# A three-pass decoder layer on one core: products with v in two groups, expert products of 512 columns, one bias product, and half of the masks added on VectorE

## The chip, the cores and the metric

One core of one Trainium2 chip. The metric is device time of one execution in microseconds (us). TensorE does matrix products and transposes, VectorE and ScalarE elementwise work and reductions, GpSimd elementwise work and the causal select; SyncE only issues transfers.

## What is computed

32 sequences of 128 tokens with 256 features, in fp32. Three residual blocks, each closed by a layer norm:

```
x = layernorm(x + causal self-attention(x))                    # 16 heads of 16
x = layernorm(x + cross-attention(x, ctx, mask))               # 16 heads of 16
x = layernorm(x + self-attention(x) + mixture(x))              # 8 experts, top 2

expert_out = einsum('bsd,edf->bsef', x, W_experts) + b_experts
mixture    = einsum('bsef,bse->bsf', expert_out, combine)      # combine: top-2 gate values, else 0
```

All 8 experts are computed for every token and weighted by `combine`.

## The kernel before

The work is cut in items of two sequences (256 tokens): 16 items, each taken through three passes (the code's layers 0, 1, 2), so n runs from 0 to 47. All tokens stay in `x_all` between the passes. The work of an item overlaps with that of its neighbours: each step has a written time in `TIMES` for each pass, an item starts `PERIOD` after the one before, and every engine's queue is the steps of its own, sorted by these times (`ORDER`, L125). Nothing is planned at run time: the order is fixed, semaphores hold each step until its inputs are there, and a step that waits holds all behind it on its engine. Only the order follows from the written times; no instruction waits for a time.

One item, in order of its data:

- x in feature-major form is split in a high part of the matmul's reduced type and a low rest (`xh`, `xl`; for ctx `ch`, `cl`). Products with weights are three passes, high x high, high x low, low x high, in `three_pass` (recorded as L429), each 128 x 128 against 256 columns.
- q and k (`q`, `k`) go through ScalarE and GpSimd into bf16 parts, which SyncE stacks by transfers in `q_stack` and `k_stack` (three buffers of each; the zeros and ones between the rows are set once at the start by `clear_stacks`, L765, on VectorE).
- First scores (`s1`, `max_scores`, L489): for each of 8 head pairs four bf16 products of 128 columns fill a bank (two banks take turns), and in the passes with a mask a fifth, identity by mask with 512 columns (L505), adds the mask. VectorE reduces the bank to four columns of negated row maxima (`max`, `row_max`, L849). When all 8 pairs are done VectorE splits the maxima in parts (`nm`, L857), TensorE transposes them (`maxt`, L513), ScalarE copies them (`mt`, L699), a transfer adds them to the stack (`ml`).
- Second scores (`s2`, `scores`, L526): transposed and with the maxima subtracted by the product; the second pass adds its mask by a product (L529). ScalarE takes the exponential (`exp`, L707) into one of four `probs` buffers; in the first pass GpSimd zeroes what lies above the diagonal (`causal`, L1004).
- Products with v (`pv`, `values`, L533): four parts per item, each of two head pairs: 16 fp32 products with 32 weight columns on four column tiles, 128 columns each. A part waits for the exponential (first pass: the causal select) of its second pair. Two parts fill a work bank, which ScalarE copies (`za`) to one of two `z_aug` buffers; TensorE transposes it (`zT`), VectorE divides by the sums (`z`).
- Passes one and two: transpose, split, output product (`zt`, `zh`, `zl`, `out`), residual and norm (`sum`, `rs`, `norm`).
- Pass three: a gate on VectorE (`gtop`, down to L844), transposed (`gateT`) and copied (`cbt`); the bias product (`bias`, L590), two fp32 products of 8 rows against 256 columns; then the experts. Unit e is expert e for both sequences: 12 products of 256 columns, `[128, 256]` per sequence (`expert`, L593); VectorE adds each sequence's half to x with its weight, two independent instructions (`combine`, L925). z is added by `zadd` (L936), then the norm.

The four work banks are handed out by `assign_banks` (L152) from the written times. Weights of later passes are loaded in eight pieces during the first two. At the start VectorE clears the three stacks, makes the first weights' low halves and the constants; ScalarE's later work waits for these constants (`setup_v`).

## Time and profile before

| | us |
|---|---|
| three runs | 1025.30 to 1025.67, median 1025.55 |
| the profiled execution, its own time | 1025.35 |
| its span | 1023.6 |
| granted TensorE clock, mean | 0.991 |

| engine | busy share | instructions |
|---|---|---|
| TensorE, products | 93% | 11008 |
| TensorE, weight loads | 80% | 11008 |
| VectorE | 75% | 2092 |
| ScalarE | 52% | 1083 |
| GpSimd | 39% | 486 |

Busy time counts an engine's instructions while they run; TensorE's are pipelined, so the distance from one start to the next is its cost in the queue, not its duration. "Idle before" is the time in which the engine had nothing running ahead of an instruction. A span contains everything from the first instruction to the last; the device time is a little longer.

### The profile page before, as it was taken

What the parts mean: (1) busy time and instruction counts of PE and PEld (TensorE: products, weight loads), DVE (VectorE), ACT (ScalarE), POOL (GpSimd) and SP (SyncE); (2) the same over time, 40 slices, a digit from 0 to 9 for tenths busy, and PEclk for the clock granted to TensorE, in tenths of its full rate; (3) what the DMA queues carried; (4) which work ended last, traced back from release to release, by engine and by line L of the source; (5) the groups of instructions that cost most, each with busy time, mean ns of one, the idle gap of its engine ahead of it and who ended that gap; (6) DMA issues with size and microseconds to landing.
All of it is one profiled execution on the core that took longest, in us unless ns stands there. A gap on an engine that the chain in (4) does not pass through costs nothing.

```text
span 1023.6 us, 28458 instructions
## 1 busy us (share of the span) xinstructions
PE 950.7 (93%) x11008; PEld 817.3 (80%) x11008; DVE 763.3 (75%) x2092; ACT 537.1 (52%) x1083; POOL 396.6 (39%) x486
## 2 busy tenths in 40 slices
PE   2889888989999999999999999999999999999996
PEld 2677777878777777877778779999999999999985
DVE  7467667677766678677676678888888888888885
ACT  3456666757665566565665654444444444444422
POOL 2567767676756243352342522222222222222200
PEclk8899999999999999999999999999999999999999
DMA  4654554545444343343342422222222222222200
GB/s 145 164 143 125 138 146 123 151 124 157 117 114 123 99 126 105 85 126 95 96 114 75 125 64 64 64 75 79 75 73 64 78 75 75 63 77 78 73 28 22
DMA packets 98134, 100.85 MB, mean 99 GB/s; under 512 B 10696, under 2 KB 90576, under 8 KB 98000
## 3 DMA queue, kind: packets, MB, share of 16 engines
q1 hardware_dynamic: 98000, 99.03, 34.9%
q8 instruction: 88, 1.44, 0.6%
q14 instruction: 46, 0.38, 0.1%
HBM read 18.51 MB, written 4.19 MB: 22 GB/s over the span
## 4 chain that ended last, share of the span: by engine, by line
PE 61%; DVE 17%; POOL 14%; issue 5%; ACT 2%; DMA 0%; DVEq 0%; POOLq 0%; ACTq 0%
PE work L429 35%; PE work L547 6%; POOL probs L1004 6%; PE scores L526 6%; PE max_scores L502 5%; DVE neg_max L849 5%; DVE x_all L901 3%; PE work L556 2%; PE max_scores L505 2%; POOL k_parts L967 2%; POOL x_all L989 2%; PE scores L529 2%; POOL q_parts L967 2%; PE work L590 2%; DVE x_all L925 1%
## 5 line engine op out<-in xcount | busy, mean ns | idle before, releaser
L849 DVE TENSOR_REDUCE neg_max<-max_scores 128x4 f32<-128x512 f32 x384 | 256.8, 683 | 105.0 <-PE max_scores L505 86.3
L707 ACT ACTIVATE probs<-scores 128x512 f32<-128x512 f32 x384 | 226.6, 596 | 202.4 <-PE scores L526 158.2
L960 POOL TENSOR_TENSOR q_full<-q_full,q_parts 128x512 f32<-128x512 f32 x48 | 56.9, 1186 | 338.7 <-ACT q_parts L663 338.7
L526 PE MATMUL scores<-q_stack,k_stack 128*128 128x128 bf16 x1536 | 151.0, 221 | 2.0 <-DMA q_stack<-neg_max_t 1.1
L502 PE MATMUL max_scores<-k_stack,q_stack 126*128 126x128 bf16 x1536 | 150.1, 220 | 1.6 <-DVE neg_max L849 1.6
L547 PE MATMUL work<-probs,v_ones 128*32 128x128 f32 x3072 | 123.7, 279 | 23.8 <-POOL probs L1004 22.3
L429 PE MATMUL work<-w_hi,split_hi 128*128 128x256 f32 (+1 forms) x448 | 138.0, 308 | 1.0
L429 PE MATMUL work<-split_hi,w_hi 128*128 128x256 f32 x384 | 118.0, 307 | 19.5 <-DVE split_lo L758 19.5
L526 PEld LDWEIGHTS scores<-q_stack,k_stack 128*128 128x128 bf16 x1536 | 97.0, 98 | 44.5 <-issue 19.2
L925 DVE SCALAR_TENSOR_TENSOR x_all<-work,combine,x_all 128x256 f32<-128x256 f32 x256 | 110.8, 474 | 27.0 <-PE work L429 24.8
L502 PEld LDWEIGHTS max_scores<-k_stack,q_stack 126*128 126x128 bf16 x1536 | 104.8, 97 | 30.0 <-issue 8.9
L429 PE MATMUL work<-w_lo,split_hi 128*128 128x256 f32 (+1 forms) x448 | 126.9, 283 | 0.0
L429 PE MATMUL work<-w_hi,split_lo 128*128 128x256 f32 (+1 forms) x448 | 126.4, 282 | 0.0
L547 PEld LDWEIGHTS work<-probs,v_ones 128*32 128x32 f32 x3072 | 72.4, 109 | 60.5 <-POOL probs L1004 26.7
L429 PE MATMUL work<-split_lo,w_hi 128*128 128x256 f32 x384 | 110.4, 288 | 0.0
L429 PE MATMUL work<-split_hi,w_lo 128*128 128x256 f32 x384 | 110.3, 287 | 0.0
L505 PE MATMUL max_scores<-mask_qk,ident_b 128*128 128x512 bf16 x256 | 97.8, 382 | 0.0
L1004 POOL TENSOR_SCALAR_AFFINE_SELECT probs<-probs 128x512 f32<-128x512 f32 x128 | 81.8, 646 | 28.0 <-ACT probs L707 26.5
L429 PEld LDWEIGHTS work<-split_hi,w_hi 128*128 128x128 f32 x384 | 75.0, 195 | 21.4 <-DVE split_lo L758 19.8
L429 PEld LDWEIGHTS work<-w_hi,split_hi 128*128 128x128 f32 x448 | 84.9, 190 | 4.4 <-DVE split_lo L761 4.1
L429 PEld LDWEIGHTS work<-w_lo,split_hi 128*128 128x128 f32 x448 | 84.9, 190 | 0.4
L429 PEld LDWEIGHTS work<-w_hi,split_lo 128*128 128x128 f32 x448 | 84.7, 189 | 0.0
(105 smaller groups left out, 2100.5 us busy)
## 6 DMA issues: line engine op xcount, KB each, us to landing
q_stack<-q_parts SPq DMA_DIRECT2D x288, 128.0 KB, 2.4
k_stack<-k_parts SPq DMA_DIRECT2D x288, 128.0 KB, 2.4
in_t<-in_xt SPq DMA_DIRECT2D x16, 256.0 KB, 2.9
x_all<-in_x SPq DMA_DIRECT2D x16, 256.0 KB, 2.9
in_t<-in_ct SPq DMA_DIRECT2D x16, 256.0 KB, 2.6
out<-x_all SPq DMA_DIRECT2D x16, 256.0 KB, 2.1
stage<-in_e SPq DMA_DIRECT2D x4, 512.0 KB, 5.2
stage<-in_qk SPq DMA_DIRECT2D x2, 512.0 KB, 4.0
```

Of the source, the lines that this page charges most:

```text
L429: mm = pe.matmul(dst, a(c), b(c), start=(c == 0 and k == 0), stop=(c == C - 1 and k == 2))
L502: mm = pe.matmul(dst[:, b, h2, :], head(QS, n, 2 * p + h2, b, ROWS), head(KS, n, 2 * p + h2, b, ROWS), start=(b + h2 == 0), stop=(b + h2 = ...
L505: mm = pe.matmul(dst[:, :, :, :], IDB[:, :], MQ[l][:, :].unsqueeze(1).to_broadcast([P, 2 * PB, P]), start=False, stop=True, skip_group_che ...
L526: mm = pe.matmul(dst[:, b, h2, :], head(KS, n, 2 * p + h2, b, rows), head(QS, n, 2 * p + h2, b, rows), start=(b + h2 == 0), stop=(b + h2 = ...
L547: mm = pe.matmul(dst[o:o + QUAD, (p % 4) * P:(p % 4 + 1) * P], VA[n % VALUES][:, b, (2 * p + h2) * VH:(2 * p + h2) * VH + QUAD], PR[S2_TUR ...
L707: act.activation(PR[g % PROBS][:, :, :, :], SS[g % 2][:, :, :, :], ACT.Exp).then_inc(probs_done, 1)
L849: dve.tensor_reduce(NM[n % 2][:, :, 2 * p:2 * p + 2], SM[g % 2][:, :, :, :], AX.X, ALU.max, negate=True).then_inc(max_read, 1)
L901: ins = dve.tensor_scalar(x[:, b, :], x[:, b, :], MV[:, l, b, 0:1], RS[:, l, b:b + 1], ALU.subtract, ALU.mult)
L925: ins = dve.scalar_tensor_tensor(out=x[:, b, :], in0=src[:, b * D:(b + 1) * D], scalar=CB[n % 2][:, b, e:e + 1], in1=x[:, b, :], op0=ALU.m ...
L960: pool.tensor_tensor(FULL[x][:, :, :], FULL[x][:, :, :], PART[x][:, 0, :, :], ALU.subtract).then_inc(rest_done[x], 1)
L967: pool.tensor_tensor(PART[x][:, 2, :, :], FULL[x][:, :, :], PART[x][:, 1, :, :], ALU.subtract).then_inc(low_done[x], 1)
L1004: pool.affine_select(probs, probs, [[0, 2 * PB], [1, P]], ALU.is_ge, 0.0, base=0, channel_multiplier=-1).then_inc(causal_done, 1)
```

## The change

Five parts, and new written times for every step (so the order of steps on each engine changes in many places; only a few are shown).

1. In passes one and two the mask product is left out for pairs 1, 3, 5 and 7. For these VectorE runs four instructions over 128 columns in place of one reduction over 512: add the mask (bf16, in SBUF) to the scores (in PSUM), times -1, running minimum into the maxima's column; the sum is written back over the scores.
2. Products with v come in two groups of four pairs. Probabilities and `z_aug` share six buffers, given out by the written times, in place of four and two.
3. An expert unit is two experts for one sequence: 6 products of 512 columns. Its two accumulations on VectorE go to the same part of x, and the second waits for the first.
4. The expert bias is multiplied in the reduced type as one product per sequence over 24 rows (high by high, high by low, low by high), in place of fp32 over 8 rows. The gate makes the three copies of its weights; the bias parts are made at the start.
5. At the start GpSimd clears the first two stacks, VectorE the third, each as 2048 words of 32 bits; TensorE runs six fp32 products of 512 columns ahead of its first work. Products with weights wait for their own low part.

```diff
+MAX_DVE = ((1, 3, 5, 7), (1, 3, 5, 7))
...
-PERIOD = [16.5, 17.99, 25.01]
+PERIOD = [16.49, 18.06, 25.0]
@@ TIMES, first pass
...
-     "max": [-16.18, -14.72, -13.26, -11.81, -10.35, -8.9, -7.45, -5.94], "nm": [-5.11], "maxt": [-4.53],
-     "exp": [0.17, 1.58, 3.0, 4.41, 5.83, 7.24, 8.66, 10.08], "pv": [3.93, 6.65, 9.36, 11.91], "za": [7.67, 12.96],
-     "norm": [31.53], "causal": [0.97, 2.38, 3.8, 5.21, 6.63, 8.04, 9.46, 10.88]},
+     "max": [-16.13, -13.83, -13.7, -12.06, -10.44, -8.46, -7.83, -4.97], "nm": [-4.02], "maxt": [-3.71],
+     "exp": [1.97, 2.98, 4.02, 4.84, 6.34, 8.28, 9.13, 9.34], "pv": [8.35, 12.36], "za": [9.01, 13.36],
+     "norm": [31.78], "causal": [3.37, 4.0, 5.26, 5.55, 7.46, 9.26, 9.62, 10.17]},
@@ TIMES, second pass
...
-     "max": [-16.26, -14.84, -13.44, -12.01, -10.59, -9.18, -7.77, -6.3], "nm": [-5.95], "maxt": [-5.21],
+     "max": [-17.1, -14.78, -13.95, -11.6, -11.1, -8.71, -7.24, -6.13], "nm": [-5.75], "maxt": [-3.27],
@@ TIMES, third pass
...
-     "rs": [23.83], "norm": [25.03], "store": [25.5]},
+     "rs": [32.15], "norm": [33.9], "store": [25.9]},
...
+ATTN_BUFS = 6
+def assign_buffers():
+    slot, before = {}, {}
+    free_at, last = [-1e9] * ATTN_BUFS, [None] * ATTN_BUFS
+    for t, kind, n, part in ORDER:
+        if kind not in ("exp", "za"):
+            continue
+        j = min((i for i in range(ATTN_BUFS) if free_at[i] <= t), key=lambda i: free_at[i])
+        slot[(kind, n, part)], before[(kind, n, part)] = j, last[j]
+        free_at[j] = WHEN[("pv", n, part // 4) if kind == "exp" else ("zT", n, part)] + 0.01
+        last[j] = (kind, n, part)
+    return slot, before
...
+            pe.wait_ge(setup_p, 1)
+            for _ in range(6):
+                pe.matmul(WB[WORK_BANKS - 1][0:QUAD, :], VA[0][:, 0, 0:QUAD], VA[0][:, :, 0:2 * P], start=True, stop=True)
...
             def max_scores(n, p):
+                added = l < 2 and p not in MAX_DVE[l]
...
-                if l < 2:
+                if added:
                     mm = pe.matmul(dst[:, :, :, :], IDB[:, :], MQ[l][:, :].unsqueeze(1).to_broadcast([P, 2 * PB, P]),
                                    start=False, stop=True, skip_group_check=True)
...
-            def values(n, j):
+            def values(n, f):
...
-                    pe.wait_ge(causal_done, S2_TURN[(n, 2 * j + 1)] + 1)
+                    pe.wait_ge(causal_done, S2_TURN[(n, 4 * f + 3)] + 1)
...
-                for p in (2 * j, 2 * j + 1):
+                for p in range(4):
...
-                    mm = pe.matmul(dst[:, b * D:(b + 1) * D], CBT[0:E, b * P:(b + 1) * P], EB[:, :], start=True, stop=True)
+                    mm = pe.matmul(dst[:, b * D:(b + 1) * D], CBT[0:BIAS_ROWS, b * P:(b + 1) * P], EBP[:, :],
+                                   start=True, stop=True)
...
-            def expert(n, e):
+            def expert(n, u):
+                g, b = divmod(u, PB)
...
+                mm = three_pass(mine("expert", n, u)[:, :],
+                                lambda c: hi[:, c, b * P:(b + 1) * P], lambda c: lo[:, c, b * P:(b + 1) * P],
+                                lambda c: wh[:, c, o:o + width], lambda c: wl[:, c, o:o + width])
...
-            clear_stacks(0).then_inc(stacks_clear, 1)
             first_low(0)
             x_low(0, 0)
-            clear_stacks(1).then_inc(stacks_clear, 1)
...
+            setup_link(dve.tensor_copy(EBH[:, :], EB[:, :]))
+            setup_link(dve.tensor_tensor(EBH[:, :], EBH[:, :].bitcast(F32), LOW_ROWS.to_broadcast([BIAS_ROWS, D]), ALU.mult))
+            dve.tensor_tensor(EBP[:, :], EB[:, :], EBH[:, :].bitcast(F32), ALU.subtract)
...
-            clear_stacks(2).then_inc(stacks_clear, 1)
+            dve.memset(pairs_of(QS[2]), 0.0)
+            dve.memset(pairs_of(KS[2]), TWO_ONES).then_inc(last_stack_clear, 1)
...
-                dve.tensor_tensor(cb[:, :, 0:E], G1[:, :, :], G2[:, :, :], ALU.add).then_inc(combine_done, 1)
+                dve.tensor_tensor(cb[:, :, 0:E], G1[:, :, :], G2[:, :, :], ALU.add)
+                dve.tensor_tensor(cb[:, :, E:2 * E], G1[:, :, :], G2[:, :, :], ALU.add)
+                link(dve.tensor_tensor(CBH[:, :, :], G1[:, :, :], G2[:, :, :], ALU.add))
+                dve.tensor_tensor(cb[:, :, 2 * E:3 * E], cb[:, :, 0:E], CBH[:, :, :].bitcast(F32),
+                                  ALU.subtract).then_inc(combine_done, 1)
...
             def row_max(n, p):
+                l = layer(n)
+                if l < 2 and p in MAX_DVE[l]:
+                    for b in range(PB):
+                        for h2 in range(2):
+                            h, scores = 2 * p + h2, SM[g % 2][:, b, h2, :]
+                            ins = dve.tensor_tensor_reduce(scores, scores, MQ[l][:, :], -1.0, HUGE, ALU.add, ALU.min,
+                                                           NM[n % 2][:, b, h:h + 1])
...
-            def combine(n, e):
+            def combine(n, u):
+                g, b = divmod(u, PB)
...
+                for half in range(2):
+                    e = 2 * g + half
+                    ins = dve.scalar_tensor_tensor(out=x, in0=src[:, half * D:(half + 1) * D], scalar=CB[n % 2][:, b, e:e + 1],
+                                                   in1=x, op0=ALU.mult, op1=ALU.add)
+                    if half == 0:
+                        link(ins)
...
@@ GpSimd, at the start
+            for j in range(2):
+                pool.memset(pairs_of(QS[j]), 0.0)
+                pool.memset(pairs_of(KS[j]), TWO_ONES).then_inc(stacks_clear, 1)
             pool.wait_ge(setup_v, 1)
```

## Rows read from the trace of the kernel before

**Rows 1.** The page's first part: busy us (share of the span) and instructions.

```profile
PE 950.7 (93%) x11008; PEld 817.3 (80%) x11008; DVE 763.3 (75%) x2092; ACT 537.1 (52%) x1083; POOL 396.6 (39%) x486
```

**Rows 2.** Windows by pass: length, busy of PE, PEld, DVE, ACT, POOL.

```profile
0.00:38.35 38.35, 16.28 (x103) 13.66 (x103) 27.06 (x35) 13.08 (x22) 11.74 (x16) 0.87 0.51 155
38.35:315.30 276.95, 250.47 (x3145) 210.74 (x3144) 187.71 (x469) 179.12 (x343) 193.85 (x252) 0.99 0.49 134
315.30:612.50 297.20, 283.59 (x3366) 228.49 (x3366) 214.92 (x525) 179.34 (x355) 111.37 (x129) 1.00 0.37 102
612.50:998.40 385.90, 383.65 (x4205) 349.64 (x4205) 320.31 (x1021) 158.97 (x353) 77.88 (x86) 1.00 0.25 69
```

**Rows 3.** Windows, same cut, of L699 alone (one per item).

```profile
612.50:998.40 385.90, 5.58 (x15) 1.00 0.25 69
```

**Rows 4.** Waits of PE in the first and the second pass: us, times, longest.

```profile
PE work L547 <- POOL probs L1004: 22.0, 20, 1.4
...
PE work L513 <- DVE neg_max_parts L858: 10.9, 14, 0.9
```

**Rows 5.** Timeline of PE in the first pass: start us, us, instruction.

```profile
253.45 0.38 PE L505 MATMUL max_scores<-mask_qk,ident_b 128*128 128x512 bf16 x1
253.67 0.39 PE L526 MATMUL scores<-q_stack,k_stack 128*128 128x128 bf16 x4
```

**Rows 6.** Timeline of PE, third pass, around products with v.

```profile
791.53 0.40 PE L502 MATMUL max_scores<-k_stack,q_stack 126*128 126x128 bf16 x4
791.86 0.65 PE L547 MATMUL work<-probs,v_ones 128*32 128x128 f32 x16
792.44 0.40 PE L526 MATMUL scores<-q_stack,k_stack 128*128 128x128 bf16 x4
792.67 0.39 PE L502 MATMUL max_scores<-k_stack,q_stack 126*128 126x128 bf16 x4
792.87 0.37 PE L429 MATMUL work<-w_hi_experts,split_hi 128*128 128x256 f32 x1
793.08 0.28 PE L429 MATMUL work<-w_lo_experts,split_hi 128*128 128x256 f32 x1
793.20 0.28 PE L429 MATMUL work<-w_hi_experts,split_lo 128*128 128x256 f32 x1
```

**Rows 7.** Windows inside that group, products with v alone.

```profile
791.85:791.95 0.10, 0.09 (x4) 0.09 (x8) 1.00 0.48 154
791.95:792.06 0.11, 0.11 (x8) 0.11 (x12) 1.00 0.26 84
```

**Rows 8.** Timeline of PE, third pass, around the bias products.

```profile
813.87 1.12 PE L590 MATMUL work<-expert_bias,combine_t 8*128 8x256 f32 x4
814.93 0.40 PE L502 MATMUL max_scores<-k_stack,q_stack 126*128 126x128 bf16 x4
```

**Rows 9.** Groups of VectorE: count | busy us, mean ns | idle.

```profile
L849 DVE TENSOR_REDUCE neg_max<-max_scores 128x4 f32<-128x512 f32 x384 | 256.8, 683 | 105.0 <-PE max_scores L505 86.3 <-PE max_scores L502 16.7
...
L925 DVE SCALAR_TENSOR_TENSOR x_all<-work,combine,x_all 128x256 f32<-128x256 f32 x256 | 110.8, 474 | 27.0 <-PE work L429 24.8
...
L870 DVE TENSOR_TENSOR z<-work,z_recip 128x128 f32<-128x128 f32 x192 | 46.9, 286 | 3.3
...
L844 DVE TENSOR_TENSOR combine<-combine_first,combine_second 128x16 f32<-128x16 f32 x16 | 2.8, 175 | 0.6
```

**Rows 10.** Timeline of VectorE in the third pass.

```profile
791.14 0.49 DVE L870 TENSOR_TENSOR z<-work,z_recip 128x128 f32<-128x128 f32 x2
...
793.01 1.28 DVE L849 TENSOR_REDUCE neg_max<-max_scores 128x4 f32<-128x512 f32 x2
```

**Rows 11.** Chain that ended last, its start: start us, us.

```profile
3.86 3.47 DVE k_stack L767
...
24.33 0.64 DVE split_lo L758
...
29.73 0.24 PE max_scores L502 x4
```

More of the change, by code:

```diff
@@ L180, in last_reader @@
 def last_reader(name, n):
-    if layer(n) == 2:
-        return "expert", n, E - 1
-    return ("q" if layer(n) == 1 and name == "x" else "v"), n, 0
+    pieces = {0: [("q", 0), ("k", 0), ("v", 0)], 1: [("q", 0)] if name == "x" else [("k", 0), ("v", 0)],
+              2: [("q", 0), ("k", 0), ("v", 1), ("expert", E - 1)]}[layer(n)]
+    kind, part = max(pieces, key=lambda piece: WHEN[(piece[0], n, piece[1])])
+    return kind, n, part
 SPLIT_BEFORE = {}
@@ L313, in bank_read, with attn, attn_free @@
             eng.wait_ge(done, n + 1 if once else turn(n) if reader == "ve" else count(reader, n, rpart))
+        def attn(kind, n, part):
+            return AT[ATTN_SLOT[(kind, n, part)]]
+        def attn_free(eng, kind, n, part):
+            use = ATTN_BEFORE[(kind, n, part)]
+            if use is None:
+                return
+            before, m, mpart = use
+            if before == "za":
+                eng.wait_ge(z_psum[mpart], m + 1)
+            else:
+                eng.wait_ge(pv_psum, PV_TURN[(m, mpart // 4)] + 1)
         def bank(kind, n, part=0):
@@ L323, in split_free @@
             kind, m, part = last_reader(*use)
-            done = {"expert": e_psum, "q": psum["q"], "v": v_psum[0]}[kind]
-            eng.wait_ge(done, count(kind, m, part) if kind == "expert" else m + 1)
+            done = {"expert": e_psum, "q": psum["q"], "k": psum["k"], "v": v_psum[part % PB]}[kind]
+            eng.wait_ge(done, count(kind, m, part) if kind == "expert" else turn(m) if kind == "v" and part else m + 1)
         def pair(n):
@@ L346, in decoder @@
         CONSTS = 5
-        S2_PIECE = {j: piece for piece, j in S2_TURN.items()}
         block = stack.enter_context(nc.Block())
@@ L502, in max_scores @@
                         mm = pe.matmul(dst[:, b, h2, :], head(QS, n, 2 * p + h2, b, ROWS), head(KS, n, 2 * p + h2, b, ROWS),
-                                       start=(b + h2 == 0), stop=(b + h2 == 2 and l == 2), skip_group_check=True)
-                if l < 2:
+                                       start=(b + h2 == 0), stop=(b + h2 == 2 and not added), skip_group_check=True)
+                if added:
                     mm = pe.matmul(dst[:, :, :, :], IDB[:, :], MQ[l][:, :].unsqueeze(1).to_broadcast([P, 2 * PB, P]),
@@ L921, in combine @@
                 for f in range(2):
[L922 removed]
+                    if WHEN[("zadd", n, f)] < WHEN[("combine", n, u)]:
                         dve.wait_ge(zadd_done[f], turn(n))
[L924 to L927 removed]
+                for half in range(2):
[4 more added lines that the diff above has]
+                        link(ins)
                 ins.then_inc(e_done, 1)
```

119 lines of the change are left out of this document (61 added, 58 removed), and 44 rows, old and new, of the table TIMES.

## The prediction

> **What bounds the kernel now.** The page's busy line gives TensorE 950.7 us of matmul in a span of 1023.6 us, VectorE 763.3, ScalarE 537.1, GpSimd 396.6 [rows 1]. The reader should not stop there: these are means over three passes. I cut the trace at the transposes of the maxima, one per item, into a start, three stretches (one per pass) and an end, and read the busy time of each [rows 2]; the same cut counts 16, 16 and 15 items, of which the last count is shown [rows 3]. So an item takes 276.95/16 = 17.3 us in the first pass, 297.2/16 = 18.6 us in the second and 385.9/15 = 25.73 us in the third; the start is 38.35 us and the end 25.2 us. VectorE is busy for 187.7/16 = 11.7, 214.9/16 = 13.4 and 320.3/15 = 21.4 us of an item, GpSimd for 193.9/16 = 12.1 us in the first pass.
>
> The waits of TensorE in those stretches say what is left over [rows 4]: in the first pass 22.0 us for the causal select on GpSimd ahead of the products with v, in the second 10.9 us for the parts of the maxima from VectorE, in the third nearly nothing (busy 383.65 of 385.9). TensorE's queue thus sets the pace everywhere: about 17.3 - 22.0/16 = 15.9 us of work per item in the first pass, 18.6 - 10.9/16 = 17.9 in the second, 25.7 in the third. What leaves its queue comes off the time, until VectorE, the next one, is full.
>
> **The masks.** In the first two passes each pair's bank of maxima scores gets four 128-column products and a 512-column product that adds the mask. From its start to the start of the next product that mask takes 253.67 - 253.45 = 0.22 us [rows 5]. Pairs 1, 3, 5 and 7 lose it: 4 x 0.22 = 0.88 us per item, 128 instructions, 28 us in all. In return VectorE does, for these pairs, four instructions over 128 columns (add the mask, negate, running minimum, sum written back to PSUM) in place of one maximum over 512. Two of those maxima back to back take 1.28 us, that is 0.64 to 0.67 each [rows 9, 10]. No row shows the new instruction. The nearest one is the 128-column multiply out of PSUM, 286 ns alone but 0.49 us for two, 0.245 each [rows 10]. The other end is the three-operand accumulation, 110.8/256 = 0.433 us over 256 columns back to back [rows 9]; with 128 columns fewer at the slope between 0.245 (128 columns) and 0.67 (512), 1.1 ns a column, it is 0.29, and its full 0.474 us bounds it above. I take 0.27: the kind is that of the first row with a second operation and an accumulator. Four are 1.08 us, 0.41 us more than the maximum, so 1.6 us per item and 53 us of VectorE in all. Bounds: 0.245 (1.2 us per item) and 0.474 (4.9 us).
>
> By the Trainium skill ("VectorE: DVE Perf Modes", on where the cycles go for N = 2048) every Vector instruction pays some 158 cycles beside its elements at 0.96 GHz, which speaks against splitting one into four: (128 + 158)/0.96 = 298 ns, 1.19 us for four, so by that estimate VectorE gets 2.1 us per item; the pair of multiplies at 0.245 us each disagrees when instructions follow one another.
>
> **The products with v.** Per item four groups of 16 become two of 32. A group of 16 takes 792.44 - 791.86 = 0.58 us to the next product's start, and the product ahead of it is at 0.33 us instead of 0.23 [rows 6]. Inside the group four column tiles start together each 0.11 us: 4 are seen in the first window and 8, four of them new, in the next [rows 7]. So 32 take about 0.58 + 4 x 0.11 = 1.02 us, against 1.16, and one entry of 0.10 goes too: 0.24 per merged group, 0.46 us per item in every pass. The wait is now for four pairs of probabilities instead of two; six shared buffers instead of four plus two hold them, and the written order puts the first product with v later (8.35 on the first pass's clock, where the causal select of the pair it needs stands at 5.55; before, 3.93 and 2.38). The distance grows from 1.5 to 2.8, and for the last group from 1.0 to 2.2. The transpose of the maxima, too, gets 2.5 behind the making of its parts in the second pass instead of 0.7. Both waits of [rows 4] should mostly go.
>
> **The experts.** A unit now is 12 products of 256 columns, 0.12 us apart (793.08 to 793.20) with 0.09 more at the first [rows 6]: 1.43 us. It becomes 6 products of 512 columns. No row has a wide product of this type; two narrow ones bound it above at 0.24, the wide bf16 mask at 0.22 is nearest and I take it: 1.32 us, 0.11 less per unit, 8 units, 0.88 us per item. The bound below is that a wide one comes at the step of a narrow one, 0.12. The two accumulations on VectorE now depend on each other and a wait stands between them; where two now take 0.87, I count 0.474 x 2 + 0.04 = 0.99: 0.12 x 8 = 0.9 us of VectorE per item (bounds 0 and 1.6).
>
> By the Trainium skill ("TensorE: Matmul & The Clock Gate", Back-to-back issue gap) a sustained stream of weight loads and products goes at about 131 ns for 512 columns. The mask in this trace takes 0.22 us and so disagrees.
>
> **The bias.** The four records of the fp32 product take 814.93 - 813.87 = 1.06 us plus an entry of 0.10 [rows 8]. Two products of 256 columns in the type of the experts are 0.24 + 0.09: 0.83 us less per item. VectorE gets three small operations and a link, at 0.175 us each [rows 9]: 0.5 us, ahead of the gate's transpose, which already stands behind other work.
>
> **Sum for the middle.** TensorE per item: first pass 15.9 - 0.88 - 0.46 = 14.6; second 17.9 - 1.34 = 16.6; third 25.7 - 0.46 - 0.88 - 0.83 = 23.6. VectorE: 11.7 + 1.6 = 13.3; 13.4 + 1.6 = 15.0; 21.4 + 0.9 + 0.5 = 22.8. In the first pass three engines now are at 12 to 14.6; before, the item took 1.09 of TensorE's work; I put 1.07 on it, since the wait for the select goes but VectorE is fuller: 15.6 (1.7 less). Second: 1.04 before, 1.03 now: 17.05 (1.55 less). Third: TensorE had no wait at all with VectorE at 83%; with VectorE at 97% of 23.6 some of VectorE's own waits for products will come through, 24.2 (1.5 less). Together 27 + 25 + 23 = 75 us. What is late next is VectorE in all three: a bank or a buffer it has not read yet.
>
> **Start and end.** The chain starts with VectorE clearing stacks: 3.47 us for one k stack alone, and the second item's low part is only made at 24.33, behind the third clearing; the first maxima scores are at 29.73 [rows 11]. Two of three clearings go to GpSimd, which is free there, and the k stack is written as 2048 words like the q stack. VectorE gets rid of two such clearings with their q stacks; the vo weights' low half, the constants and the third clearing (3.47 us at most, both stacks now at half of that each) remain, with three bias operations of under 0.5 us each. The six new fp32 products on ones ahead of the first q: a 256-column fp32 product takes 0.53 here, so six of 512 columns take at least 6.4 us, up to 12.7 at half clock, from about 2 us on: they may hold q back to 8 to 14 us, but keep the engine busy, and q and k come out at full clock instead of half. I take 8 us off the start (4 to 12). The end I leave as it is.
>
> The sum is against the profiled execution, 1025.35 us (span 1023.6 and 1.75 around it), which is 0.2 us under the median of 1025.55: 1025.35 - 75 - 8 = 942, and I say 943.
>
> **Rivals.** (a) TensorE stays the only bound and all its waits go: periods 14.8, 16.6 and 23.6, with 12 us at the start: 40 + 32 + 32 + 12 = 116, so 909; halfway there 918. For it: the longer distances in the written order. Against: VectorE over 90% in every pass.
>
> (b) VectorE becomes the bound: the new instruction at 0.34 adds 2.7 us per item, so 14.4 and 16.1, with waits 16.4 and 17.7, and 24.8 in the third: 14 + 14 + 14 + 6 = 48, so 977. For it: four instructions in place of one, each with a write to PSUM that no row prices.
>
> (c) Slower: the new instruction is as dear as a 256-column one or dearer. It decides from where passes one and two lose what the third and the start give, 31 us, one us per item: 18.3 and 19.6 with VectorE at 97%, 17.75 and 19.0 of work, less 11.7 and 13.4, plus the 2.68 of four removed maxima, over 16: 0.52 to 0.55 us each. At 0.6: 11.7 + 6.9 = 18.6 and 20.3, over 0.97: 19.2 and 20.9, 67 us more, less 31: 1061. Against it: no 128-column row is near that.
>
> (d) The wide products come at the narrow step of 0.12: the unit is 0.72 us, TensorE has 5 us per item less in the third pass, VectorE's 22.8 decides at 23.5: 2.2 x 15 = 33 instead of 23, so 933. The Trainium skill's 131 ns ("TensorE: Matmul & The Clock Gate", Back-to-back issue gap) would be near this case.
>
> (e) The wide product gains nothing (0.24) and the start nothing: 943 + 13 + 8 = 964 at most, inside (b)'s reach.
>
> **How the numbers follow.** Forecast (930 to 960) 0.44, (a) 0.17, (b) with (e) 0.28, (c) 0.05, (d) 0.03, and 0.03 for an order that blocks somewhere and eats most of it. The range leaves out part of (a), (c) and the last: 915 to 982. A change of 0.2% is what a measurement here can tell from none. Faster 0.92, same 0.02, slower 0.06.
>
> **What would show it.** Items of 15.6, 17.05 and 24.2 us between transposes of the maxima; the new instruction at 0.27 us back to back; 0.22 us between wide products; groups of 32 at 1.0 us; TensorE's waits for the causal select and the maxima's parts a few us in all, and new short ones for VectorE; first maxima scores near 22 us. Items above 17.3 us in the first pass with VectorE without idle time would prove me wrong.

## The result: 988.49 us, faster, and 45 us above the forecast

The changed kernel takes 988.49 us (median of 4 runs, 973.48 to 989.21) against 1025.61 for the kernel before beside it (4 runs, 1025.30 to 1026.11): 3.6% less. The ratio on record, 0.956 with the 95% interval 0.944 to 0.968, counts only the two runs within 1.5% of the fastest, 973.48 and 987.90 (median 980.69), though the other two, 989.08 and 989.21, differ from 987.90 by hardly more than 0.1% and have its granted clock. I had said 943 (915 to 982): the median of all four lies above that range, the 980.69 just inside it, and this by one execution. The profiled execution took 987.9 us, span 986.2.

The run of 973.48 granted a mean clock of 0.985 instead of 0.966. That is 2 x 0.015 x 972 = 29 us at half clock instead of 2 x 0.034 x 986 = 67, and start and end alone have 24 us of it in the profiled execution. So most of the 13 falls of the clock that are described below should be missing in it (an estimate from the two means; this run has no profile).

The page's first part and its clock row; the columns are those of [rows 1].

```profile
PE 916.7 (93%) x10092; PEld 764.5 (78%) x10092; DVE 841.0 (85%) x3035; ACT 538.0 (55%) x1083; POOL 408.7 (41%) x490
...
PEclk8899999999999999999999999999999999999999
```

TensorE lost 916 products and 34 us of busy time, VectorE gained 943 instructions and 78 us. The windows of the changed kernel, cut as in [rows 2] at ScalarE's copies of the transposed maxima (the copy is what [rows 3] counts, not the transpose itself); after the busy times come the granted clock, the DMA share and GB/s.

```profile
0.00:38.35 38.35, 24.60 (x127) 17.15 (x128) 19.01 (x62) 14.41 (x25) 18.69 (x20) 0.79 0.59 183
38.35:283.80 245.45, 231.45 (x3093) 202.74 (x3091) 225.11 (x923) 174.84 (x342) 194.99 (x253) 1.00 0.53 148
283.80:557.50 273.70, 265.58 (x3287) 221.11 (x3287) 230.69 (x943) 180.49 (x354) 115.14 (x128) 1.00 0.40 110
557.50:961.80 404.30, 379.20 (x3439) 311.63 (x3440) 352.78 (x1065) 161.85 (x352) 78.09 (x86) 0.95 0.24 67
961.80:986.20 24.40, 15.83 (x150) 11.88 (x150) 13.40 (x44) 6.39 (x12) 1.77 (x4) 0.90 0.07 23
```

Divided by 16, 16 and 15 items: 15.34 us an item in the first pass (forecast 15.6), 17.11 in the second (17.05), 26.95 in the third (24.2; before 25.73). Against [rows 2] that is -31.5, -23.5, **+18.4**, nothing at the start and -0.8 at the end. Two passes came as forecast; the third, which was to give 23 us, costs 18. The granted clock says where to look: 1.00 in passes one and two, 0.95 in the third.

Waits of TensorE, columns as in [rows 4]: first pass, second pass, third pass.

```profile
PE max_scores L562 <- DVE neg_max L918: 5.8, 8, 1.4
PE work L573 <- DVE neg_max_parts L930: 5.4, 12, 0.5
```

```profile
PE max_scores L562 <- DVE neg_max L918: 3.7, 13, 0.4
```

```profile
PE work L650 <- DVE combine_t L979: 22.8, 15, 1.7
```

The 22.0 us for the causal select and the 10.9 for the parts of the maxima in [rows 4] are gone, as forecast, and short waits for VectorE stand in their place. In the third pass, which had next to none, TensorE now waits once per item, 1.5 us, for a copy on VectorE (the gate's transpose, which the new bias product reads). Behind that wait the clock falls. TensorE in one item of the third pass (start us, us, instruction, wait ahead of it), and then windows across one item and its two falls:

```profile
762.41 0.38 PE L643 MATMUL work<-consts,combine 128*32 128x128 f32 x2
762.72 1.08 PE L607 MATMUL work<-attn,v_ones 128*32 128x128 f32 x32
765.41 0.46 PE L650 MATMUL work<-expert_bias_parts,combine_t 24*128 24x256 f32 x2 [1.61 <-DVE combine_t L979]
765.81 0.40 PE L562 MATMUL max_scores<-k_stack,q_stack 126*128 126x128 bf16 x4
...
767.84 0.77 PE L477 MATMUL work<-w_hi,split_hi 128*128 128x512 f32 x1
```

```profile
738.90:742.30 3.40, 3.40 (x21) 3.11 (x19) 2.44 (x9) 1.09 (x2) 0.06 (x1) 0.51 0.76 201
742.30:766.20 23.90, 22.20 (x214) 17.99 (x214) 21.41 (x65) 9.97 (x22) 5.50 (x6) 1.00 0.18 51
766.20:769.60 3.40, 3.40 (x21) 3.10 (x18) 2.48 (x8) 1.09 (x2) 0.02 (x1) 0.51 0.76 202
```

For 3.4 us the granted clock is 0.51, the lower level of 1.2 GHz, and the same wide product takes 0.77 us instead of 0.40. It begins 0.8 us after the engine resumed from 1.61 us without work (0.2 to 1.0 us over the whole pass), and it comes 13 times, once per item: twelve items of 27.27 us and the short last one, against 25.69 in the one full item without a fall. That item has the same wait of 1.61 us.

Why the copy was late stands on VectorE's timeline of the same item, and beside it GpSimd's:

```profile
761.28 1.00 DVE L999 SCALAR_TENSOR_TENSOR x_all<-work,combine,x_all 128x256 f32<-128x256 f32 x2
762.19 0.68 DVE L921 TENSOR_REDUCE neg_max<-max_scores 128x4 f32<-128x512 f32 x1
762.79 1.55 DVE L973 TENSOR_SCALAR x_all<-x_all,mean_var,rstd 128x256 f32<-128x256 f32 x2
764.26 0.68 DVE L921 TENSOR_REDUCE neg_max<-max_scores 128x4 f32<-128x512 f32 x1
764.86 0.40 DVE L979 CAST combine_t<-work 32x256 fp32r<-32x256 f32 x1
```

```profile
762.71 1.16 POOL L1045 TENSOR_TENSOR q_parts<-q_full,q_parts 128x512 bf16<-128x512 f32 x1 [2.55 <-ACT q_parts L731]
```

The copy stands in VectorE's written order behind an earlier item's norm (L973) and a maximum: on this item's clock the norm of the item two before is at 33.9 - 50 = -16.1, the maximum at -16.07 and the copy at -15.54. What it copies left TensorE at about 762.8 (762.41 + 0.38), the copy starts at 764.86, and TensorE's next instruction but one needs it. The norm is long besides: 1.55 us for two instructions that take 0.72 elsewhere (below), while a GpSimd instruction is running; those 0.83 us are about half of the wait. The gate's own small step (L901) shows it at the full size, 0.28 us in most places and

```profile
758.91 1.28 DVE L901 TENSOR_SCALAR combine_first<-consts,gate_index_f,gate_top 128x8 f32<-128x8 f32 x1
```

with a GpSimd instruction of 1.16 us from 759.00 to 760.16 beside it: VectorE's ends with it. In the third pass 14 of the 30 steps of L901 are of 1.20 to 1.28 us, and each has such a GpSimd instruction beside it; the 16 of 0.28 or 0.29 have none. The Trainium skill ("SBUF — State Buffer", Who interferes with whom) says that VectorE and GpSimd share one pair of SBUF ports under an exclusive lock; that agrees with these rows.

### The profile page after: what moved, and what is told of

It is laid out like the page before. It is cut to its first block, busy times and chain, and to the rows that moved or that the text cites. A ratio compares the mean times of both kernels' runs of the same rounds, so it can differ in the third digit from the quotient of the medians.

```text
span 986.2 us, 27881 instructions
## 1 busy us (share of the span) xinstructions
PE 916.7 (93%) x10092; PEld 764.5 (78%) x10092; DVE 841.0 (85%) x3035; ACT 538.0 (55%) x1083; POOL 408.7 (41%) x490
## 4 chain that ended last, share of the span: by engine, by line
DVE 49%; PE 34%; issue 9%; ACT 5%; POOL 2%; DMA 1%; SPq 0%; DVEq 0%; POOLq 0%; ACTq 0%
PE work L477 19%; DVE neg_max L921 8%; DVE x_all L999 7%; DVE max_scores L918 6%; DVE x_all L973 3%; PE work L616 3%; DVE bn_stats L955 3%; PE max_scores L562 3%; PE scores L586 3%; PE work L607 3%; DVE combine_first L901 2%; DVE neg_max_parts L929 2%; DVE neg_max L918 2%; DVE x_all L965 2%; DVE v_ones L879 1%
## 5 line engine op out<-in xcount | busy, mean ns | idle before, releaser
L767 ACT ACTIVATE attn<-scores 128x512 f32<-128x512 f32 x384 | 219.7, 598 | 135.7 <-PE scores L586 122.7
L921 DVE TENSOR_REDUCE neg_max<-max_scores 128x4 f32<-128x512 f32 x256 | 174.0, 680 | 19.9 <-PE max_scores L565 18.9
L918 DVE CUSTOM_DVE_ANT_0 max_scores<-max_scores,mask_qk 128x128 f32<-128x128 f32 x512 | 132.3, 320 | 1.6 <-PE max_scores L562 1.6
L477 PE MATMUL work<-w_hi,split_hi 128*128 128x256 f32 (+2 forms) x320 | 118.0, 369 | 0.0
L477 PE MATMUL work<-w_lo,split_hi 128*128 128x256 f32 (+2 forms) x320 | 107.9, 337 | 0.0
L477 PE MATMUL work<-w_hi,split_lo 128*128 128x256 f32 (+2 forms) x320 | 107.1, 335 | 0.0
L607 PE MATMUL work<-attn,v_ones 128*32 128x128 f32 x3072 | 103.8, 275 | 1.7 <-ACT attn L767 0.8
L607 PEld LDWEIGHTS work<-attn,v_ones 128*32 128x32 f32 x3072 | 78.5, 109 | 21.9 <-issue 19.7
L1082 POOL TENSOR_SCALAR_AFFINE_SELECT attn<-attn 128x512 f32<-128x512 f32 x128 | 86.0, 689 | 17.7 <-ACT attn L767 17.6
L773 ACT ACTIVATE attn<-work 128x512 f32<-128x512 f32 x96 | 57.0, 593 | 49.3 <-PE work L607 49.3
```

The source lines that it names most:

```text
L477: mm = pe.matmul(dst, a(c), b(c), start=(c == 0 and k == 0), stop=(c == C - 1 and k == 2))
L607: mm = pe.matmul(dst[o:o + QUAD, p * P:(p + 1) * P], VA[n % VALUES][:, b, h * VH:h * VH + QUAD], attn("exp", n, 4 * f + p)[:, 2 * b + h2, ...
L767: act.activation(attn("exp", n, p)[:, :, :], SS[g % 2][:, :, :, :].rearrange("k b h q -> k (b h) q"), ACT.Exp).then_inc(probs_done, 1)
L773: act.activation(attn("za", n, f)[:, :, :].rearrange("p k q -> p (k q)"), bank("pv", n, f)[:, :], ACT.Copy).then_inc(za_done[f], 1)
L918: ins = dve.tensor_tensor_reduce(scores, scores, MQ[l][:, :], -1.0, HUGE, ALU.add, ALU.min, NM[n % 2][:, b, h:h + 1])
L921: ins = dve.tensor_reduce(NM[n % 2][:, :, 2 * p:2 * p + 2], SM[g % 2][:, :, :, :], AX.X, ALU.max, negate=True)
```

## The experiments

**1. The norm and the store.** The times of the written order are moved, one at a time. In the third pass the norm goes behind the copy:

```diff
-     "rs": [32.15], "norm": [33.9], "store": [25.9]},
+     "rs": [32.15], "norm": [35.2], "store": [25.9]},
```

> The changed kernel with one written time moved: the third pass's norm at 35.2 instead of 33.9, so VectorE copies the gate's transpose (combine_t) ahead of the 1.55 us of norm instead of behind it. Theory: the 1.6 us in which TensorE waits for that copy is what costs the third pass its gain, both as time and because the granted clock falls to half for 3.4 us behind each such wait (1.7 us more). Then items of the third pass take 27.3 - 1.6 - 1.7 = 24.0 us, the clock is 0.98 or more, and the whole 943 us. Rival: VectorE is full in the third pass (352.8 of 404.3 us busy), the wait shows up at another place and the clock falls as before: 980 to 990 us, clock 0.966.

956.85 us (955.56 to 959.77), ratio 0.933 (0.931 to 0.935); items 15.35, 17.13 and 24.85; the wait for the copy falls from 22.8 us to 1.3 and the granted clock of the third pass is 1.00. One number of the order was worth 31.6 us (988.49 - 956.85, and the same between the third passes of the two traces, 404.3 - 372.7). The wait and the clock went as expected; the 943 did not come, for the items are 24.85 and not 24.0, 13 of the 14 us between. A new wait of 5.2 us (9 times) for the row of maxima in the q stack is left. It comes from SyncE's queue, whose orders run one behind the other: it waits with the store for the norm, and the next item's stacks stand behind it, then the row of maxima. SyncE of this kernel in the third pass, waits, then timeline:

```profile
SPq L447 <- DVE x_all L973: 216.1, 14, 17.0
```

```profile
700.91 0.38 SPq L447 DMA_DIRECT2D out<-x_all  x1
701.38 4.74 SPq L430 DMA_DIRECT2D q_stack<-q_parts  x6
```

So the store is moved behind the norm as well:

```diff
-     "rs": [32.15], "norm": [35.2], "store": [25.9]},
+     "rs": [32.15], "norm": [35.2], "store": [35.9]},
```

> e1_norm_later with the third pass's store written at 35.9 instead of 25.9, behind its norm: SyncE's queue stands 15.5 us per item at that store, then issues 12 stack transfers in one go and the maxima's transfer last, for which TensorE waits 5.2 us in 13 items. Theory: that wait goes and the items come to 24.2 to 24.5 us from 24.85: 947 to 951 us against 956.9. Rival: TensorE's queue is full at 24.07 us of busy time and the burst is hidden: 955 to 957 us.

**949.81 us** (949.56 to 951.15), ratio 0.926 (0.925 to 0.928): the best version, faster than both kernels. Items 15.35, 17.17 and 24.41, start 37.5. Its windows (passes one, two, three) and, in the third pass, VectorE around the copy, which now goes ahead of the norm:

```profile
37.50:283.10 245.60, 231.30 (x3093) 202.39 (x3091) 224.96 (x923) 174.83 (x341) 194.88 (x253) 1.00 0.53 147
283.10:557.80 274.70, 266.50 (x3287) 221.48 (x3288) 231.27 (x943) 180.31 (x354) 115.25 (x128) 1.00 0.40 110
557.80:923.90 366.10, 358.90 (x3439) 293.33 (x3440) 329.18 (x1064) 161.74 (x352) 78.38 (x86) 1.00 0.27 74
```

```profile
771.99 0.40 DVE L979 CAST combine_t<-work 32x256 fp32r<-32x256 f32 x1
772.33 0.72 DVE L973 TENSOR_SCALAR x_all<-x_all,mean_var,rstd 128x256 f32<-128x256 f32 x2
```

**2. Wait or clock.** Two kernels put seven unread 512-column products (1.6 us) into each item of the third pass of the changed kernel: the one at the bias product, ahead of its wait, the other ahead of the first group of products with v.

```diff
             def expert_bias(n, part):
-                pe.wait_ge(gt_done, turn(n))
                 dst = mine("bias", n)
+                wh, _, o, width = piece_to["e0"]
+                for _ in range(7):
+                    pe.matmul(dst[:, :], source(n)[0][:, 0, 0:P], wh[:, 0, o:o + width], start=True, stop=True)
+                pe.wait_ge(gt_done, turn(n))
```

> The changed kernel, with seven products of 512 columns that nobody reads put ahead of the bias product's wait, 7 x 0.233 = 1.6 us: TensorE works where it waited. The wait itself stays. Theory (the clock falls because TensorE stands still there): no falls of the clock in the third pass, items of 27.3 - 1.7 = 25.6 us, whole 988 - 13 x 1.7 = 966 us. Rival (the falls have to do with the narrow products around, or with time since the last fall): clock 0.966 as before and 988 us.

```diff
                 dst = mine("pv", n, f)
+                if l == 2 and f == 0:
+                    for _ in range(7):
+                        pe.matmul(dst[:, :], WHE[:, 0, 0:P], WHE[:, 0, 0:2 * D], start=True, stop=True)
```

> The changed kernel with seven products of 512 columns that nobody reads put ahead of the first group of products with v of each third-pass item, into that group's bank: 7 x 0.233 = 1.6 us of work directly ahead of the place where TensorE stands still for combine_t. Theory: the work takes the place of the standing still (the copy on VectorE comes no later), so the items lose only the fall of the clock: 27.27 - 1.6 = 25.7 us, like the few items of the changed kernel behind which the clock did not fall; 963 to 967 us, clock 0.99. Rival (the clock falls for what follows the wait, not for the wait): falls as before, 987 us. Second rival (the fillers only push the wait back): 27.3 us per item with the clock at 0.99.

The first missed its place: the bias's bank is set free by the same copy, so TensorE stood still first and the unread products came on top of the wait. 993.81 us, ratio 0.969 (0.967 to 0.970), items of 27.23 in the third pass. It still tells something: its third pass waits

```profile
PE work L650 <- DVE combine_t L982: 19.9, 14, 1.5
```

at a granted clock of 1.00. A wait of 1.5 us alone does not bring the fall. The kernel of the third experiment, whose third pass is unchanged, says the same without an added product: TensorE stands still 14 times for 1.6 us in it, and behind four of these waits the clock does not fall. One of the four, and the window around it:

```profile
824.58 0.47 PE L650 MATMUL work<-expert_bias_parts,combine_t 24*128 24x256 f32 x2 [1.61 <-DVE combine_t L979]
```

```profile
824.00:850.00 26.00, 24.00 (x230) 19.64 (x230) 23.64 (x73) 11.21 (x25) 5.59 (x7) 1.00 0.26 73
```

The wait is thus what the falls of this pass stand behind, but a wait of the same length can stand without one. The second did what it was for: 970.82 us (968.71 to 972.04), ratio 0.947 (0.945 to 0.948). Windows of its third pass:

```profile
555.60:941.00 385.40, 383.12 (x3544) 311.94 (x3545) 347.18 (x1065) 160.39 (x353) 78.58 (x86) 1.00 0.25 70
```

It has no fall of the clock and no wait for the copy. Its items are 25.70 us, as long as the changed kernel's one full item without a fall (25.69): seven unread products cost nothing against the wait that they fill. Only in the pass's first item, where there was no such wait to fill, they cost 1.3 us. The third pass thus splits into four: 404.3 - 385.4 = 18.9 us for the clock's falls (thirteen at 27.27 - 25.70 = 1.57 us are 20.4, less those 1.3), 385.4 - 372.7 = 12.7 for the wait, net of what other waits take back (372.70 is the same stretch of the kernel with the norm alone moved), 372.7 - 366.1 = 6.6 for the store, and 366.1 is left, where 24.2 x 15 = 363 was forecast.

**3. The masks.** All mask products are given back to TensorE, in the changed kernel (first) and in the best one (second); the edit is the same.

```diff
-MAX_DVE = ((1, 3, 5, 7), (1, 3, 5, 7))
+MAX_DVE = ((), ())
```

> The changed kernel with all masks added by TensorE again (no pair on VectorE), the rest and the order kept. Theory (TensorE's queue still sets the pace in passes one and two, VectorE at 92% and 84% just keeps up): TensorE gets back 0.88 us per item, 15.34 becomes 16.1 and 17.1 becomes 17.8, 23 us more in all: 1010 us. Rival (VectorE is the bound there, since the masks cost it 4 x (1.60 - 0.67) = 3.7 us per item): the first two passes stay as they are or gain, 980 to 988 us.

> e6_norm_store with all masks added by TensorE. From e3_masks_on_pe (items of 15.36 and 17.34 us against 15.34 and 17.11): 0.02 x 16 + 0.23 x 16 = 4 us more, 954 us. Rival (the forecast's 0.88 us per item from TensorE's queue): 28 us more, 978 us.

982.88 us (975.87 to 990.46), ratio 0.957 (0.950 to 0.964), items 15.36 and 17.34. That it is 5.6 us under the changed kernel says nothing of the masks: its traced execution has 10 falls of the clock in the third pass instead of 13. In the best version 950.96 (949.92 to 952.19), ratio 0.9275 (0.9259 to 0.929), items 15.31 and 17.34. So this part is worth nothing in the first pass and 0.2 us per item in the second, 1.2 us of 950 in the medians, which lies inside the runs' spread. The numbers nearest to it are those of the first expectation's rival. Its reason holds in part: VectorE, busy for 92% and 84% of the best version's first two passes, hands the saving back as waits, but both its price (0.40 us for the new instruction, see below) and "the bound" were too much. The windows of the second kernel's passes one and two show how:

```profile
35.30:280.30 245.00, 239.90 (x3152) 208.12 (x3150) 210.20 (x475) 174.83 (x342) 194.63 (x253) 1.00 0.53 149
280.30:557.70 277.40, 274.54 (x3347) 228.35 (x3348) 210.97 (x523) 181.72 (x354) 114.52 (x128) 1.00 0.40 108
```

Beside the best version's windows, TensorE is busy 8.6 us longer in the first pass (0.54 per item) and the pass is no longer: what the removed products save comes back as waits. TensorE's first-pass waits for VectorE are 5.7 and 5.4 us in the best version, for the maxima and for their parts, as in the changed kernel (above). In this one only this is left of them:

```profile
PE max_scores L562 <- DVE neg_max L921: 1.8, 4, 0.6
```

The opposite edit gives all eight pairs to VectorE, in the best version:

```diff
-MAX_DVE = ((1, 3, 5, 7), (1, 3, 5, 7))
+MAX_DVE = ((0, 1, 2, 3, 4, 5, 6, 7), (0, 1, 2, 3, 4, 5, 6, 7))
```

> e6_norm_store with all eight pairs' masks on VectorE in passes one and two: four more pairs, 4 x (1.60 - 0.67) = 3.7 us more of VectorE and 0.88 us less of TensorE per item. Theory (VectorE is at 14.1 and 14.4 us of busy time per item and becomes the bound at 17.8 and 18.1): items of 18.2 and 18.6 us, 16 x (2.9 + 1.5) = 70 us more than e6_norm_store. Rival (TensorE's queue still decides): 10 to 28 us less.

957.57 us (955.88 to 958.08), ratio 0.933 (0.931 to 0.934), items 15.65 and 17.29: 8 us more, not 70, and the rival's gain did not come either; VectorE is now busy for 95% of the first pass (237.35 of 250.40 us). The price that I had put on the new instruction in this expectation was wrong. A group's busy sums gave 0.32 us for it and 0.14 for the reading of its accumulator, and I had added them up; the timeline shows that they overlap and that the next one starts 0.25 us after the last (changed kernel, second pass):

```profile
330.08 0.33 DVE L918 CUSTOM_DVE_ANT_0 max_scores<-max_scores,mask_qk 128x128 f32<-128x128 f32 x1
330.33 0.13 DVE L918 DVE_READ_ACCUMULATOR2_ANT neg_max<- 128x1 f32 x1
330.33 0.33 DVE L918 CUSTOM_DVE_ANT_0 max_scores<-max_scores,mask_qk 128x128 f32<-128x128 f32 x1
```

**4. Parts alone in the kernel before.** The masks part alone, in the order as it was:

```diff
+                if l < 2 and p in MAX_DVE:
...
+                            ins = dve.tensor_tensor_reduce(scores, scores, MQ[l][:, :], -1.0, HUGE, ALU.add, ALU.min,
+                                                           NM[n % 2][:, b, h:h + 1])
```

> The kernel before with the masks part alone: pairs 1, 3, 5, 7 of passes one and two add their mask on VectorE, order and all else as before. Theory (in the changed kernel the part brings 0.2 us an item or less, because VectorE at 0.40 us per new instruction loses 3.7 us an item and hands back waits): between 1012 and 1026 us, pass one near 17.1 and pass two near 18.3 us. Rival (TensorE's queue alone counts, 0.88 us per item): 1025.6 - 28 = 998 us. Second rival: the old order has the maxima on the path, 1035 us or more.

1062.36 us (1059.14 to 1064.0), ratio 1.035 (1.033 to 1.038), items 18.04, 20.04 and 25.74: each earlier pass is slower than with the mask products. Waits in the first and in the second pass, then the windows of both passes:

```profile
PE work L550 <- POOL probs L1015: 23.8, 19, 1.6
```

```profile
PE work L516 <- DVE neg_max_parts L869: 24.8, 13, 2.0
```

```profile
39.60:328.20 288.60, 249.03 (x3091) 211.20 (x3095) 210.17 (x918) 178.15 (x343) 192.28 (x254) 0.97 0.47 128
328.20:648.90 320.70, 289.94 (x3303) 236.63 (x3295) 236.43 (x945) 178.53 (x355) 110.83 (x127) 0.94 0.35 95
```

The old order has the transpose of the maxima only 0.7 behind its parts, and with a fuller VectorE it waits 24.8 us (10.9 before), and the clock falls here too, 4 and 11 times, to a mean of 0.97 and 0.94. VectorE is far from full: 210.17 of 288.60 us. The products with v in two groups of 32 alone (with five buffers of probabilities; the first pass's times are shown, the other two change alike):

```diff
-... "pv": [3.93, 6.65, 9.36, 11.91], "za": [7.67, 12.96],
+... "pv": [6.65, 11.91], "za": [7.67, 12.96],
...
-PROBS = 4
+PROBS = 5
```

> The kernel before with the products with v alone in two groups of four pairs, at the written times of the old second and fourth group, five buffers of probabilities (all that fits) instead of four; order and all else as before. Theory (a merged group saves one entry and one end, 0.23 us, two per item, and half of the points where TensorE waits for the causal select go): pass three 25.73 - 0.46 = 25.3, pass two 18.1, pass one 16.3 us; 1025.6 - 7 - 7 - 16 = 996 us. Rival (the group waits for two more pairs and the saving comes back as waits): 1015 to 1035 us.

1040.26 us (1039.83 to 1045.62), ratio 1.016 (1.013 to 1.019), items 18.85, 18.16 and 25.53. The second pass gives 0.42 us per item (0.46 was worked out), the third 0.2, and the first loses 1.5. The group of 32 stands where the second group of 16 stood and needs the same select, so this is not what it waits for. What is new is a wait of ScalarE, which the kernel before does not have: with five buffers the sixth pair's exponential can start only when the first group has read the first pair's, up to 2.4 us later, and the selects that the second group needs are late with it. TensorE's waits in the first pass (us 40 to 320), then ScalarE's:

```profile
PE work L547 <- POOL probs L1004: 31.2, 16, 2.2
```

```profile
ACT probs L707 <- PE work L547: 34.1, 15, 2.4
```

The clock falls 8 times in this pass (once in the kernel before), a mean of 0.95, which should be part of the 1.5 us. So this kernel prices the group together with too few buffers; with the changed kernel's six it was not tried in the old order.

**5. The experts.** Each unit goes back to 12 products of 256 columns, with the norm moved as in the first experiment.

```diff
-                mm = three_pass(mine("expert", n, u)[:, :],
...
+                for half in range(2):
+                    q = o + half * D
+                    mm = three_pass(dst[:, half * D:(half + 1) * D],
```

> As e1_norm_later (third pass's norm at 35.2), but each expert unit as 12 products of 256 columns into the two halves of its bank in place of 6 of 512; same units, same order. Theory (wide products come 0.233 us apart, narrow ones 0.119, so width saves 0.005 us a pair): 0.24 us per item more than e1_norm_later, 4 us in all. Rival (fewer weight loads matter beyond the distance of the starts): 0.1 us per unit, 13 us more.

960.38 us (959.34 to 960.92), ratio 0.936 (0.934 to 0.937), third pass 25.09 against 24.85: 0.24 us per item, 3.5 us in all, as expected. (One of its items in the trace has a fall of the clock, so 0.24 is, if anything, too much.)

**6. The start.** In the best version the three bias operations get a semaphore of their own and move behind the third clearing; and, in another kernel, the six fp32 products on ones are left out.

```diff
-        CONSTS = 5
+        CONSTS = 4
+        eb_loaded = sem("eb_loaded")
...
-            for _ in range(6):
-                pe.matmul(WB[WORK_BANKS - 1][0:QUAD, :], VA[0][:, 0, 0:QUAD], VA[0][:, :, 0:2 * P], start=True, stop=True)
```

> e6_norm_store with the start changed: VectorE's constants no longer wait for the transfer of the expert bias (it had waited 3.4 us for it), and the three bias operations (1.2 us) stand behind the clearing of the third stack. Theory (the changed kernel's start is held by this wait: first maxima scores at 25.7 us, the first transpose of maxima at 37.5 to 38.4 us as before the change): 3 to 4 us less, 946 us. Rival (VectorE clears, splits and reduces behind it in the same time and the half-clock stretches of the start decide): within 1 us of e6_norm_store, 949.8 us.

> e6_norm_store without the six fp32 products ahead of TensorE's first work. They run from 1.9 to 8.8 us and hold back q and k, whose inputs are ready at 7.3 us, by 1.5 us, but these then come 0.117 us apart instead of 0.213. Theory (both are hidden behind VectorE's constants, until 13.2 us): within 1 us of 949.8 us. Rival (the clock that they bring early moves the later half-clock stretches): 2 to 5 us more.

950.39 us (949.9 to 952.2), ratio 0.927 (0.925 to 0.929), and 950.05 (948.38 to 952.09), ratio 0.927 (0.925 to 0.928), with starts of 38.5 and 37.0. Neither makes a difference: the same start took 36.2 to 38.4 us in the traces of the kernels above. In the first the constants still waited until 10.06 us, now for another transfer.

## Why the prediction was right and where it failed

**Passes one and two: right, but not by the terms of the sum.** 15.34 and 17.11 against 15.6 and 17.05. The group of 32 takes 1.01 us to the next start (1.02 forecast) and the new instruction 0.25 (0.27). But the sum let the mask products bring 0.88 us per item, and they bring 0 and 0.2; VectorE's waits return the rest. That the total came near all the same is luck in this term. The best version with all masks on TensorE takes 245.0 + 277.4 = 522.4 us for the two passes, the best version itself 520.3 and the kernel before 574.2 [rows 2]. So 51.8 of the 53.9 us come without the masks part. Of these, 32.1 are idle time of TensorE that went (length less busy time: 40.1 in the kernel before, 8.0 in the one with all masks on TensorE), and 19.6 are busy time. What is left to bring them is the written order with its longer distances, which removed the waits of [rows 4], and the merged groups (0.46 us for 32 items would be 15 of the 19.6); this is by exclusion. The parts alone in the old order lose 36 and 15 us. How much the order alone would give, no run separates: it was not tried with four groups and all masks.

**Third pass: the step that failed** is "VectorE gets three small operations and a link [...] 0.5 us, ahead of the gate's transpose, which already stands behind other work". The operations cost about what was said. That all of this has cover is what I had wrongly assumed: the copy of the transposed gate, not the operations ahead of it, is what the new bias product waits for, at a place where only one group of products with v, 1.0 us, lies between. I had counted instructions and not followed the one value VectorE hands back. The price is the wait and, behind it, the clock at half, 12.7 and 18.9 us, and the store's place on SyncE, 6.6 us, a queue that the prediction did not walk. With the order mended the item takes 24.41 us, near the 24.2.

That nearness has two errors in it. The wide product was taken at 0.22 us, the mask's step; in the changed kernel's third pass three steps take 0.70 us, 0.233 each (two products are left out here),

```profile
757.22 0.40 PE L477 MATMUL work<-w_hi,split_hi 128*128 128x512 f32 x1
...
757.92 0.40 PE L477 MATMUL work<-w_hi,split_hi 128*128 128x512 f32 x1
```

so two narrow ones (two steps of 0.12, [rows 6]) are hardly longer: 0.24 us per item instead of 0.88 (the fifth experiment). The bias product takes 765.81 - 765.41 = 0.40 against 1.06 in [rows 8], 0.66 less, near the 0.83. Altogether TensorE's busy time fell from 383.65/15 = 25.58 us per item [rows 2] to 358.90/15 = 23.93, by 1.65 where the sum had 2.17; these two terms alone miss 0.64 and 0.17, and what made up for 0.3 of that no run shows. The 0.6 us that I set aside for VectorE's waits was near: in the best version TensorE has 366.1 - 358.9 = 7.2 us without work in the pass, 0.48 per item, 0.35 of it in waits that have a releaser, its 22 us of VectorE per item (329.18/15) notwithstanding.

**The start** was to be 8 us shorter and is the same. The first maxima scores come at 25.5 us, 4 us earlier than in [rows 11] (22 forecast), but the first transposed maxima are copied at 38.4 as before, where the start is cut. The transpose itself comes 1.2 us earlier than before (36.88 against 38.11), and its copy then stands behind the third item's k in ScalarE's written order:

```profile
36.88 0.40 PE L573 MATMUL work<-ident_b,neg_max_parts 128*32 128x128 bf16 x2
```

```profile
38.40 0.36 ACT L761 ACTIVATE neg_max_t<-work 32x256 bf16<-32x256 bf16 x1
```

TensorE is busy in the start for 24.60 us instead of 16.28 [rows 2], and the clock is at half in two stretches. The early products, then the first products at 20.22, and the windows of the two stretches:

```profile
1.94 6.88 PE L483 MATMUL work<-v_ones 128*32 128x512 f32 x12 [1.94 <-POOL v_ones L1029]
...
20.22 0.58 PE L477 MATMUL work<-split_hi,w_hi 128*128 128x256 f32 x1 [8.38 <-DVE split_lo L820]
```

```profile
15.30:25.60 10.30, 5.38 (x25) 5.29 (x26) 4.49 (x3) 4.03 (x8) 4.99 (x5) 0.50 0.70 198
...
32.40:39.20 6.80, 5.52 (x27) 5.10 (x28) 3.24 (x20) 1.74 (x4) 0.63 (x1) 0.50 0.59 181
```

The 24 products of the first q and k do come at full clock, as I had said, but TensorE then has no work for 8.38 us, and the next 24 come at half. Apart from ScalarE's order at its very end, what decides these 38 us stays open; the transfer of the bias and the early products do not.

**The rivals.** (a) is right that TensorE stays the bound, with VectorE busy for 329.18 of the best version's 366.1 us, but its waits do not all go: 15.35, 17.17 and 24.41 in that version against its 14.8, 16.6 and 23.6 (and halfway between its 909 and the 943 is 926, not the 918 given there). (b) and (c) did not come, for the new instruction was cheaper than forecast. That the measured time lies near (b)'s 977 is chance: its first two passes (16.4 and 17.7) are wrong. Nor is the masks part alone in the old order a case of (c), though it is slower: VectorE is busy for 73% of the first pass there, and it is the waits of that order that grow. (d) fell with 0.233 us. (e) is right in both of its halves, the wide product and the start, 21 us of the 45 that the forecast missed. The 0.03 left for "an order that blocks somewhere and eats most of it" is nearest to what happened in the third pass, and that is where the range was too narrow: it ended at 982 and the median of all four runs is 988.

## What to carry to other kernels

When an operation is rewritten, follow the value that comes back from the other engine: where it is made, what stands ahead of it in that engine's order, and how much work the waiting engine has until then. A wait of 1.6 us once per item cost 31.6 us in 15 items of the traced execution, more than half of it through the clock that fell behind it; look at the granted clock first when a pass is longer than its busy time explains. And a queue that runs in order, a DMA queue too, has to be walked for every moved step: one store that waited 15 us per item held the next item's stacks back.

## What the runs showed of the hardware

- A 512-column product in the experts' type starts 0.233 us after the last, a 256-column one 0.117: per column the same, and joining them saved 0.24 us per item of 48 pairs.
- The masked maximum with its accumulator takes 0.25 us per 128 columns back to back from PSUM, though its records sum to 0.46.
- The granted clock fell to half for 3.4 us after TensorE resumed from 1.6 us without work, behind 13 of 14 such waits in one trace and behind 10 of 14 in another with the same third pass, and 3.4 us at half cost 1.57 us. With 1.5 us without work and 1.6 us of unread 512-column products behind the wait there was none. What tells these apart is not settled, and executions of one kernel differ by it: 973.48 to 989.21 us.
- Unread products in the place of a wait kept the clock up and cost nothing where there was a wait to fill: 970.82 against 988.49 us.
- A VectorE TENSOR_SCALAR of 0.28 us took 1.28 beside a GpSimd instruction, and two of 0.72 together took 1.55.
